# Four neighbouring steps side by side in the one-hots and products of a graph kernel's build

## What is computed

```python
# layer 0: scores = (Q[src] . K[dst]) * sigmoid(sum(edge_attr)); mean over dst of V[dst] * scores
# layer 1: agg = segment_sum(x[src], dst)
# layer 2: two rounds of agg = segment_sum(x[src] * ew[:, None], dst)
# layer 3: attention with a softmax over the edges of each dst
```

## Time and profile before

| | us |
|---|---|
| median of 3 executions | 7298.62 (7296.18 to 7300.44) |
| the profiled execution, its own time | 7304.09 |
| its span in the profile | 7302.2 |
| PE busy over the span | 5696.5 (78%) |
| DVE busy | 3871.9 (53%) |
| ACT busy | 2399.0 (33%) |
| POOL busy | 1846.6 (25%) |
| L1546, the products: 2352 instructions | 1650.6 busy, 764 ns each |
| L1080, the build's matmuls: 14112 | 1840.4 busy |
| L1115, the layers' matmuls: 19208 | 2255.5 busy |

### The profile page before, as it was taken

One profiled execution on the slowest core, in us unless ns is written; L12 is line 12 of the kernel. 1 busy time (PEld: TensorE's weight loads), 2 busy tenths in 40 slices (PEclk: granted clock), 3 DMA queues, 4 the chain that ended last, 5 costly groups with the idle time before them and its releaser, 6 DMA issues.

```text
span 7302.2 us, 165142 instructions
## 1 busy us (share of the span) xinstructions
PE 5696.5 (78%) x48472; PEld 4870.7 (67%) x48472; DVE 3871.9 (53%) x9331; ACT 2399.0 (33%) x7252; POOL 1846.6 (25%) x1782
## 2 busy tenths in 40 slices
PE   1777777777777779999999999998166666656665
PEld 0666666666666679999999999998144444444444
DVE  6999999999999942221111111112144444444444
ACT  2666666666666621111110000002022222222222
POOL 2000000000000010000000000001777777777771
PEclk9999999999999999999999999998577777777776
DMA  6777777777777786666766767673222222222221
GB/s 188 301 296 303 295 300 296 302 301 300 297 299 297 298 297 266 254 267 270 279 277 275 282 272 281 274 278 116 47 59 60 61 60 60 60 61 60 60 59 32
DMA packets 260785, 1540.75 MB, mean 211 GB/s; under 512 B 56235, under 2 KB 86965, under 8 KB 233836
## 3 DMA queue, kind: packets, MB, share of 16 engines
q1 hardware_dynamic: 201380, 1406.77, 49.1%
q0 software_dynamic: 59008, 129.85, 7.4%
q10 hardware_dynamic: 130, 0.80, 0.0%
HBM read 795.75 MB, written 743.08 MB: 211 GB/s over the span
## 4 chain that ended last, share of the span: by engine, by line
PE 48%; DVE 21%; issue 12%; POOL 12%; ACT 3%; DMA 2%; ACTq 1%; DVEq 0%; SPq 0%; another core or an unknown queue 0%; POOLq 0%
PE psum L1115 30%; DVE field L1546 13%; POOL field L809 11%; PE psum L1080 6%; PE psum L1304 3%; PE psum L1282 3%; DVE field L1539 1%; ACT field L923 1%; ACT field L1011 1%; DVE field L1540 1%; DVE field L1541 1%; DMA field<-head_table,cmp 1%; DVE work L1843 1%; DVE work L1850 1%; DMA field<-in_edge_attr 1%
## 5 line engine op out<-in xcount | busy, mean ns | idle before, releaser
L1115 PE MATMUL psum<-field 128*128 128x128 f32 x19208 | 2255.5, 277 | 25.5 <-issue 18.5
L1115 PEld LDWEIGHTS psum<-field 128*128 128x128 f32 x19208 | 2232.7, 189 | 26.0 <-issue 18.7
L1080 PE MATMUL psum<-field 128*128 128x200 bf16 (+1 forms) x14112 | 1840.4, 274 | 200.5 <-DVE field L1546 188.5
L923 ACT COPY field<-psum x4704 | 1654.8, 415 | 791.6 <-PE psum L1080 724.9
L1546 DVE TENSOR_TENSOR field<-field 128x1176 bf16<-128x1176 bf16 x2352 | 1650.6, 764 | 0.0
L809 POOL DMA_INDIRECT field<-head_table,cmp x1563 | 1504.6, 963 | 476.3 <-issue 470.8
L1080 PEld LDWEIGHTS psum<-field 128*128 128x128 bf16 x14112 | 1048.6, 99 | 470.6 <-issue 224.4
L1071 PE MATMUL psum<-zero_b 128*128 128x2 bf16 x4704 | 796.9, 169 | 315.4 <-ACT field L923 308.6
L1071 PEld LDWEIGHTS psum<-zero_b 128*128 128x128 bf16 x4704 | 464.3, 99 | 473.9 <-issue 401.2
L753 POOL DMA_INDIRECT field<-tile_rows,step_t_i x74 | 213.8, 2890 | 2222.4 <-PE psum L1051 2173.0
L1011 ACT COPY field<-psum x1611 | 432.0, 268 | 1044.7 <-PE psum L1304 743.5
(11 more groups left out here) (289 smaller groups left out, 2587.7 us busy)
## 6 DMA issues: line engine op xcount, KB each, us to landing
adj<-field SPq DMA_DIRECT2D x882, 800.0 KB, 5.1
field<-adj SPq DMA_DIRECT2D x196, 3200.0 KB, 10.0
field<-head_table,cmp POOLq DMA_INDIRECT x1563
field<-in_edge_attr SPq DMA_DIRECT2D x4, 3072.0 KB, 27.1
head_table<-field SPq DMA_DIRECT2D x7, 476.0 KB, 3.2
tile_rows<-field SPq DMA_DIRECT2D x1, 3328.0 KB, 18.6
right_edges<-zeros SPq DMA_DIRECT2D x1, 3328.0 KB, 20.0
place_rows<-right_edges SPq DMA_DIRECT2D x25, 128.0 KB, 2.8
```

The lines of the kernel that those rows point to most:

```text
L923: act.copy(evac[:, :, bass.ds(place, SEG)], build_banks[:, bass.ds(bank, NSEG * SEG)].rearrange("p (w c) -> p w c", w=NSEG)).then_inc(pair ...
L1080: mm = pe.matmul(build_banks[:, bass.ds(cur[j % ROUND], end - first)], hot, pr[:, first:end], start=False, stop=True, skip_group_check=True)
L1115: mm = pe.matmul(ps_y[slot][:, 0:D], source[:, hi, :], adj_in[slot][:, :, 2 * hi:2 * hi + 2], start=(hi == 0), stop=(hi == NB - 1))
```

## The change

In `prod`, `place_hot` and `iota_b` the last dimension s becomes `SIDE` = 4: four neighbouring steps lie together. A batch of eight steps then has two groups in place of four pairs. The comparisons keep their number and their elements, with patterns of 2 groups of four in place of 4 pairs. The products are two instructions a batch of 2352 elements each, in place of four of 1176. PE reads each step's columns with a stride of four elements (8 bytes). `iota_b` takes twice the space, and the cast that fills it writes 512 elements a partition in place of 256. Waits and semaphores stay as they are.

```diff
+SIDE = 4
...
-        prod = [piece(BATCH * (1 + 2 * PARTS) * SEG // 2).bitcast(BF16).rearrange("p (q c s) -> p q c s", q=BATCH // 2, s=2) for _ in range(2)]
-        place_hot = [piece(BATCH * P // 2).bitcast(BF16).rearrange("p (q c s) -> p q c s", q=BATCH // 2, s=2) for _ in range(2)]
+        prod = [piece(BATCH * (1 + 2 * PARTS) * SEG // 2).bitcast(BF16).rearrange("p (q c s) -> p q c s", q=BATCH // SIDE, s=SIDE) for _ in range(2)]
+        place_hot = [piece(BATCH * P // 2).bitcast(BF16).rearrange("p (q c s) -> p q c s", q=BATCH // SIDE, s=SIDE) for _ in range(2)]
...
-        iota_b = piece(P).bitcast(BF16).rearrange("p (c s) -> p c s", s=2)
+        iota_b = piece(P * SIDE // 2).bitcast(BF16).rearrange("p (c s) -> p c s", s=SIDE)
...
-                    pair, odd = j % BATCH // 2, j % 2
-                    hot, pr = place_hot[buf][:, pair, :, odd], prod[buf][:, pair, :, odd]
+                    side, lane = j % BATCH // SIDE, j % SIDE
+                    hot, pr = place_hot[buf][:, side, :, lane], prod[buf][:, side, :, lane]
...
-            c.then(dve.tensor_copy(iota_b, iota[:, :].rearrange("p (c s) -> p c s", s=1).to_broadcast([P, P, 2])))
+            c.then(dve.tensor_copy(iota_b, iota[:, :].rearrange("p (c s) -> p c s", s=1).to_broadcast([P, P, SIDE])))
...
-                        return tab[:, field, at:at + BATCH].rearrange("p (q a s) -> p q a s", a=1, s=2).to_broadcast([P, BATCH // 2, m, 2])
+                        return tab[:, field, at:at + BATCH].rearrange("p (q a s) -> p q a s", a=1, s=SIDE)\
+                            .to_broadcast([P, BATCH // SIDE, m, SIDE])
...
-                        return iota_b[:, 0:m, :].rearrange("p (a c) s -> p a c s", a=1).to_broadcast([P, BATCH // 2, m, 2])
+                        return iota_b[:, 0:m, :].rearrange("p (a c) s -> p a c s", a=1).to_broadcast([P, BATCH // SIDE, m, SIDE])
...
-                    for q in range(BATCH // 2):
+                    for q in range(BATCH // SIDE):
                         parts = pr[:, q, 0:COUNT_AT, :].rearrange("p (k c) s -> p k c s", c=SEG)[:, :, 0:HI2, :]
-                        s0 = at + 2 * q
+                        s0 = at + SIDE * q
                         ins = dve.tensor_tensor(parts, first[:, q, :, :].rearrange("p (a c) s -> p a c s", a=1)
-                                                .to_broadcast([P, VALUES, HI2, 2]),
-                                                tab[:, 0:VALUES, s0:s0 + 2].rearrange("p k (a s) -> p k a s", a=1)
-                                                .to_broadcast([P, VALUES, HI2, 2]), ALU.mult)
+                                                .to_broadcast([P, VALUES, HI2, SIDE]),
+                                                tab[:, 0:VALUES, s0:s0 + SIDE].rearrange("p k (a s) -> p k a s", a=1)
+                                                .to_broadcast([P, VALUES, HI2, SIDE]), ALU.mult)
                     ins.then_inc(batch_ready, 1)
```

## The result

| | before | after |
|---|---|---|
| median, us | 7301.66 (7296.18 to 7305.02, 6 runs) | 7988.98 (7987.66 to 7991.98, 6 runs) |
| span of the profiled execution, us | 7302.2 | 7990.1 |
| PE busy, us | 5696.5 | 6904.9 |
| DVE busy, us | 3871.9 | 3827.6 |

The ratio is 1.0943, with a 95% interval of 1.0929 to 1.0957: 687 us slower. The range said 7200 to 7288. Behind the build the two executions take the same time: DVE starts the last of its 588 batches at 2605 us before and at 3293 us after, which is the whole difference.

What follows compares the result with a forecast made beforehand. DVE was taken to bound the build. Of 82 us of DVE time saved, 54 reach the end: 7304.1 - 54 = 7250, less 5.5 for the median against the profiled execution, 7244.6, stated as 7244; range 7200 to 7288.

Steps and rivals of the forecast that it cites:

- Step (a): DVE's products in the build: two of 2352 elements for four of 1176 save 0.14 us a batch, 82 us of DVE time.
- Step (d): PE's reads in the build at 8 bytes instead of 4: claimed to cost nothing, with 0.26 us a step as the end.
- Step (e): Share of DVE's saving reaching the build's end: 0.74 us a chunk after waits for PE, 54 us in all.
- The pauses I had added to PE's chunk: PE in each build chunk: four pauses while registers load, 1.36 us each, 5.4 us together.
- PE as the bound of the build: Rival: PE's reads at new 16-byte places lengthen build steps; 294 us more, 7593, or 900 more at full price; chance 0.14.
- my own sum for PE: PE's need per build chunk: steps 21.8, register pauses 5.4, transposes 0.74, low clock 1.2; 29.1 of DVE's 32.7 us.
- the slow clock: Rival: PE's shorter pause at the split avoids low-clock stretches in the build; 41 us more gained, 7204; chance 0.15.
- the eaten gain: Rival: slightly longer PE steps in the build, 0.034 us each, eat the 0.74 us a chunk: 7290 to 7310; chance 0.13.

Runs made afterwards that it cites:

- DVE's part alone: Kernel before, pair layout kept, two product instructions a batch over two pairs each, value table kept pair by pair: 7234.7 us, ratio 0.9907.

## Why the prediction was wrong

**Step (a)**, the products' price, was right to the hundredth: 2.59 us for two, a batch of 3.74 us wherever PE keeps up.

**Step (d)** failed: "I take nothing, since each place of 16 bytes still gives two columns, as in L1115". Measured, it is 0.32 us a step (0.656 less 0.34), above even the dear end of 0.26 that I had kept. The mistake is in how I used the row. L1115 does hop for free, but at its own slow pace. Its matmuls follow each other every 0.115 us, as this piece of the chain that ended last shows for the kernel before (start, us, what):

```profile
2650.42 5.51 PE psum L1115 x48
```

For 128 columns that is 0.9 ns a column, 1.8 ns for each place, since a place gives two of them. The build's columns come every 0.48 ns, so the new layout asks for a place every 0.96 ns. A row that shows one place per 1.8 ns says nothing of one per 0.96. The old layout, four columns to a place, asks for one per 1.9 ns by the same reckoning. Taken from start to start of two neighbouring matmuls, as in the runs above, the old layout asks for one per 1.8 ns. So both rows sat at the very edge of what the runs show (1.8 ns a place), and I took them for rows with room to spare. Put in places per time, the trace of before had no row on the cheap side at all, and the term's honest range reached from nothing to double.

The Trainium skill (SBUF — State Buffer, "Specifications (TRN2)") asks for two or more reads of a line of 16 bytes for full bandwidth, and adds a penalty for each change of line. For PE's moving operand two are not enough, and the measurement decides: two bf16 columns of a line run at half the pace of four (0.93 against 0.48 ns a column).

**Step (e)** could not come true, since PE had become the bound: no slow-clock stretch is left, no register pause, and next to no wait for DVE. The pauses I had added to PE's chunk (5.4 us) vanish once PE never runs dry, and yet 64 steps and the transposes alone make 42.9. Where PE keeps up, the step holds: DVE's part alone gave 65 us where it said 54, and moving the transposes gave 20.6 where it said that the wait costs 0.3 us a chunk, 22 in all.

**The rivals.** The one on the other side, PE as the bound of the build, is what happened, with its place and its sign right. Its low chance of 0.14 came from L1115, read wrongly. Its price was too low: 294 us, and 900 at the outer end, against 687. I had the price of a hop (0.38 ns) from a weight load that never was the limit; the runs show 0.93 - 0.48 = 0.45 ns for every column, not for every second one. That 687 lies between the two prices is partly luck: 0.32 us a step put into my own sum for PE, 29.1 + 64 x 0.32 = 49.6 us a chunk, would have given 1190 us, and only the pauses that vanish bring it down. The rivals on the slow clock and on the eaten gain could not decide anything in the kernel after, where no stretch at the lower clock is left; with DVE's part alone the slow-clock rival came true in part.

## What to carry to other kernels

For a strided read by PE, work out how many 16-byte places a nanosecond the operand asks for, from the distance between the starts of neighbouring matmuls, and compare that with the fastest such demand in the trace, not with any row that has a hop. A layout that allows one engine a longer instruction can be paid for by the other engine that reads it: try first to merge the instructions by reordering the small operand (here the table of values), which brought the whole of DVE's forecast gain and left PE's reads alone. And when a producer's wait comes once per period, look at what its consumer does before the step that frees the buffer; moving that by seven steps gave 20.6 us, nearly a third of what the merged instructions gave.

## What was not expected of the hardware

- PE's moving operand costs about 1.8 ns per place of 16 bytes once PE's columns ask for places faster than that (0.18 us for 100 places, 0.36 for 198). Steps of 0.34, 0.34, 0.42, 0.515 and 0.96 us at 2, 4, 6, 8 and 16 bytes between columns, and 0.97 at 32.
- Neighbouring pairs do not help: 0.515 us a step with two columns side by side in each place, the same as 8 bytes apart.
- PE's weights bear the stride of 8 bytes for 118 instead of 99 ns a load, nearly all of it hidden behind the matmuls.
- DVE reads and writes runs of two and of four bf16 at the same pace: 2352 elements in 1.295 us either way (2.59 for two, in the kernel after and in the one with pairs).
